# Causal mask inside the vector instruction of the row maxima, and two query tiles scaled ahead of the sine product of the queries, in an attention and soft-expert kernel

## What is computed

```python
q = rope(einsum('bim,mhd->bhid', x, wq)); k = rope(einsum('bim,mhd->bhid', x, wk))
s = einsum('bhid,bhjd->bhij', q, k) / D_HEAD
s = s - INFTY_APPROX * (i < j)              # causal mask: 1e30 where the key is later than the query
p = softmax(s, axis=-1)
o = einsum('bhij,bhjd->bhid', p, v)
x = layernorm(x + einsum('bhid,hdm->bim', o, wo))
```

## Time and profile before

| | us |
|---|---|
| median of 3 runs (lowest, highest) | 2020.32 (2019.03, 2022.83) |
| the profiled execution | 2017.05 |
| its span | 2015.3 |
| PE busy | 1873.9 |
| DVE busy | 1481.6 |
| ACT busy | 1237.2 |
| POOL busy | 1168.8 |

### The profile page before, as it was taken

One profiled execution on the slowest core, in us unless ns is written; L12 is line 12 of the kernel. 1 busy time (PEld: TensorE's weight loads), 2 busy tenths in 40 slices (PEclk: granted clock), 3 DMA queues, 4 the chain that ended last, 5 costly groups with the idle time before them and its releaser, 6 DMA issues. The chain is left out here.

```text
span 2015.3 us, 37894 instructions
## 1 busy us (share of the span) xinstructions
PE 1873.9 (93%) x11126; PEld 1512.8 (75%) x11134; DVE 1481.6 (74%) x2670; ACT 1237.2 (61%) x2543; POOL 1168.8 (58%) x996
## 2 busy tenths in 40 slices
PE   5999999999999999999999999999999968999997
PEld 4777777777777777777777777777777756887886
DVE  4777777777777777777777777777777766777774
ACT  4666666666666666666666666666666644554553
POOL 3666666666666666666656666666666653445543
PEclk8999999999999999999999999999999989999999
DMA  6222322232223222322232223222322230111100
GB/s 201 56 55 86 107 55 55 86 107 55 55 86 107 55 55 86 107 55 55 86 107 55 55 86 107 55 55 86 96 55 55 86 126 22 33 46 38 31 21 22
DMA packets 75415, 142.98 MB, mean 71 GB/s; under 512 B 7936, under 2 KB 42880, under 8 KB 73088
## 3 DMA queue, kind: packets, MB, share of 16 engines
q1 hardware_dynamic: 74208, 141.65, 24.4%
q10 hardware_dynamic: 1184, 1.05, 0.2%
HBM read 16.52 MB, written 8.39 MB: 12 GB/s over the span
## 5 line engine op out<-in xcount | busy, mean ns | idle before, releaser
L397 POOL TENSOR_SCALAR probs<-probs,inv 128x1024 f32<-128x1024 f32 (+7 forms) x514 | 518.5, 1020 | 525.0 <-DVE inv L533 522.2
L432 ACT ACTIVATE probs<-ps_slot,neg_max 128x1024 f32<-128x1024 f32 (+7 forms) x514 | 379.4, 743 | 153.5 <-DVE neg_max L525 153.3
L689 PE MATMUL ps_turn<-ident,probs 128*128 128x128 f32 x2304 | 338.9, 279 | 78.2 <-POOL probs L397 69.4
L525 DVE TENSOR_REDUCE neg_max<-ps_slot 128x1 f32<-128x1024 f32 (+7 forms) x514 | 377.7, 756 | 31.3 <-PE ps_slot L666 20.2
L689 PEld LDWEIGHTS ps_turn<-ident,probs 128*128 128x128 f32 x2304 | 249.9, 141 | 129.3 <-issue 94.5
L664 PE MATMUL ps_slot<-k,q 128*128 128x512 f32 (+3 forms) x772 | 303.2, 393 | 0.0
L659 PE MATMUL ps_slot<-k,q 128*128 128x512 f32 (+3 forms) x772 | 285.8, 370 | 10.1 <-DVE q L551 9.9
L666 PE MATMUL ps_slot<-k,q 128*128 128x512 f32 (+3 forms) x772 | 267.4, 346 | 0.0
L452 ACT ACTIVATE pt_split<-ps_turn 128x512 fp32r<-128x512 f32 x256 | 153.5, 600 | 131.1 <-PE ps_turn L689 129.1
L386 POOL TENSOR_TENSOR rot_k<-unrot_k,rope 128x1024 f32<-128x1024 f32 x64 | 158.1, 2470 | 86.5 <-ACT unrot_k L438 86.5
L558 DVE TENSOR_TENSOR pt_split<-ps_turn,pt_split 128x512 fp32r<-128x512 f32 x256 | 176.2, 688 | 36.8 <-ACT pt_split L452 30.3
(11 more groups left out here) (175 smaller groups left out, 4108.8 us busy)
## 6 DMA issues: line engine op xcount, KB each, us to landing
swapped_q<-unrot_q SPq DMA_DIRECT2D x130, 256.0 KB, 3.8
swapped_k<-unrot_k SPq DMA_DIRECT2D x130, 256.0 KB, 4.5
x_in<-x_t SPq DMA_DIRECT2D x18, 1024.0 KB, 4.6
w_in<-w_all SPq DMA_DIRECT2D x65, 256.0 KB, 2.3
xw_in<-x_whole SPq DMA_DIRECT2D x18, 512.0 KB, 5.7
wvo_in<-wvo_all SPq DMA_DIRECT2D x65, 64.0 KB, 1.9
x_rows<-in_L_attn_x SPq DMA_DIRECT2D x8, 512.0 KB, 5.1
y_t<-y_out SPq DMA_DIRECT2D x8, 512.0 KB, 2.7
```

The source lines that it names most:

```text
L397: pool.tensor_scalar(tile, tile, inv[:, par, stat_col[t]:stat_col[t] + 1], 1.0, ALU.mult, ALU.mult).then_inc(normed, 1)
L432: last = act.activation(probs[:, p_at[t]:p_at[t] + width[t]], src, ACT.Exp, bias=neg_max[:, par, c:c + 1], accum_out=sums[:, par, c:c + 1])
L525: dve.tensor_reduce(neg_max[:, par, c:c + 1], slot(fill, par)[:, i * BANK:i * BANK + width[t]], AX.X, ALU.max, negate=True).then_inc(maxed, 1)
L689: last = pe.transpose(ps_turn[:, bank, at:at + P], probs[:, p_at[t] + j * P:p_at[t] + (j + 1) * P], ident[:, :])
```

## The change

The mask's product on PE and its two bf16 constants are gone. In their place `causal`, a bf16 row of 1024 columns that is 0 and has -1e30 above the diagonal of its last 128 columns, is an operand of `rowmax`: one DVE instruction adds its last 128(t+1) columns to a tile's scores, negates, writes the result back to PSUM and takes the minimum. ACT's exponential has `scale=-1.0` to undo the sign. DVE's wait for `filled` stands in an instruction of its own (`wait_apart`) and DVE waits once for the constants. On POOL, `norm(head_no, par, 4)` moves ahead of `mul_sin(0, head_no + 2)`.

```diff
+        causal = s.sb("causal", [P, T], BF16)
...
+            pool.memset(causal[:, :], 0.0).then_inc(consts, 1)
...
+            pool.affine_select(out=causal[:, T - P:T], in_=causal[:, T - P:T], compare_op=ALU.is_ge, fill=MASKED,
                                base=0, pattern=[[-1, P]], channel_multiplier=1).then_inc(consts, 1)
...
                 norm(head_no, par, 3)
                 mul_sin(1, head_no + 2)
+                norm(head_no, par, 4)
                 mul_sin(0, head_no + 2)
-                norm(head_no, par, 4)
                 norm(head_no, par, 5)
...
-                    last = act.activation(probs[:, p_at[t]:p_at[t] + width[t]], src, ACT.Exp,
+                    last = act.activation(probs[:, p_at[t]:p_at[t] + width[t]], src, ACT.Exp, scale=-1.0,
                                           bias=neg_max[:, par, c:c + 1], accum_out=sums[:, par, c:c + 1])
...
-                dve.wait_ge(filled, head_no * FILLS + fill)
+                wait_apart(dve, filled, head_no * FILLS + fill, dve_ticks)
                 for i, t in enumerate(SLOT_TILES[slot_no]):
                     c = stat_col[t]
-                    dve.tensor_reduce(neg_max[:, par, c:c + 1], slot(fill, par)[:, i * BANK:i * BANK + width[t]],
-                                      AX.X, ALU.max, negate=True).then_inc(maxed, 1)
+                    tile = slot(fill, par)[:, i * BANK:i * BANK + width[t]]
+                    dve.tensor_tensor_reduce(tile, tile, causal[:, T - width[t]:T], -1.0, UNSEEN,
+                                             ALU.add, ALU.min, neg_max[:, par, c:c + 1]).then_inc(maxed, 1)
...
+            dve.wait_ge(consts, 5)
             mul_cos_q(1)
...
-                        if c0 + n == width[t]:
-                            pe.matmul(out[:, n - P:n], ident_b[:, :], mask_b[:, :], start=False, stop=False,
-                                      skip_group_check=True)
```

More of the change, by code:

```diff
@@ L29 @@
 MASKED = -1e30
+UNSEEN = 3e38
 LN_EPS = 1e-5
@@ L245, in attention_block @@
         ident = s.sb("ident1", [P, P], F32)
-        ident_b = s.sb("ident_b", [P, P], BF16)
-        mask_b = s.sb("mask_b", [P, P], BF16)
+        causal = s.sb("causal", [P, T], BF16)
         zeros_b = s.sb("zeros_b", [P, BANK], BF16)
@@ L251, in attention_block @@
         ps_y = s.ps("ps_y", [P, 2, BANK])
-        consts, ticks = s.sem("consts"), s.sem("ticks")
+        consts, ticks, dve_ticks = s.sem("consts"), s.sem("ticks"), s.sem("dve_ticks0")
         x_rows_landed, x_turned = s.sem("x_rows_landed"), s.sem("x_turned1")
@@ L371, in _ @@
             pool.memset(ident[:, :], 0.0).then_inc(consts, 1)
-            pool.memset(ident_b[:, :], 0.0).then_inc(consts, 1)
-            pool.memset(mask_b[:, :], 0.0).then_inc(consts, 1)
+            pool.memset(causal[:, :], 0.0).then_inc(consts, 1)
             pool.memset(zeros_b[:, :], 0.0).then_inc(consts, 1)
             pool.memset(y_out[:, :], 0.0).then_inc(y_free, 1)
[L377 to L381, removed]
+            pool.wait_ge(consts, 3)
+            pool.affine_select(out=ident[:, :], in_=ident[:, :], compare_op=ALU.not_equal, fill=1.0,
+                               base=0, pattern=[[-1, P]], channel_multiplier=1).then_inc(consts, 1)
+            pool.affine_select(out=causal[:, T - P:T], in_=causal[:, T - P:T], compare_op=ALU.is_ge, fill=MASKED,
                                base=0, pattern=[[-1, P]], channel_multiplier=1).then_inc(consts, 1)
@@ L717, in _ @@
             project_v(FIRST, F_V0, 0, 1)
-            pe.wait_ge(consts, 7)
+            pe.wait_ge(consts, 5)
             pe.wait_ge(lo_made[K_ALL], 1)
```

## The result

The changed kernel takes 2187.57 us (median of 4 runs, 2186.57 to 2189.19). The kernel before, run on the same chip, takes 2019.67 us (4 runs, 2018.35 to 2022.83). The ratio is 1.083, with a 95% interval of 1.0811 to 1.0848. The forecast was 2150 in a range from 2070 to 2205; the sign and the places were right, the sum was 38 us short.

A forecast was written before the change was run, and what follows sets the result against it. The prediction took a loop through POOL, DVE, ACT and PE in every head as the bound, not PE alone. 2017 profiled + 76 late chain + 54 clock = 2147, with 3 for the median 2150 us; range 2070 to 2205.

The forecast's parts named there:

- The order on POOL: POOL's queries' product ends 1.9 us later, DVE's keys' sum waits for it; scores +1.65 us a head before masks.
- Where PE stands: PE stands 1.1 us before turn 5 and 1.75 before the scores of slot 0, with 0.7 of work between.
- a small wait of the scores for `q`: Sign of a wrong forecast: PE's wait for DVE's `q` small, so the exclusion or the reciprocal's time is misread.
- The other heads: Last two heads of each batch, 16 in all: between +0.35 and 1.37 us, taken as 0.6 each, 10 us.
- The new instruction: DVE's maxima: the pass costs nothing more, 0.1 us a tile for the second instruction; 6 us in all at 0.2.
- The clock: PE's longer stands bring the lower clock in half the heads, 32 x 1.7 = 54 us; bounds 0 to 109.
- the usual heads: 48 heads whose scores of slot 0 start 1.37 us later, masks taken off: 66 us.
- the masks' own gain: Only the masks of tiles 7 and 6 lie on the loop at PE: 0.28 us a head less.
- B: Rival: the same late chain of keys and queries, but PE's clock stays up; 2096 us, chance 0.24.
- C: Rival: DVE's sum of the keys gets ahead of POOL's queries' product; +0.8 us a head, 2071 us, chance 0.1.
- D: Rival: DVE's new instruction runs at half the rate, about 2.6 us a head more; over 2260 us, chance 0.05.

The follow-up runs named there:

- e3_filled: The changed kernel plus nine products of a zero tile per head where PE stands, four ahead of turn 5, five ahead of its second bank: 2114.11 us.
- e1_join_only: The changed kernel with POOL's old order, both sine products ahead of the scaling of tiles 1 and 0, keeping the joined mask: 2011.44 us.
- e5_queries_only_written: The changed kernel with POOL's sine product of the queries replaced by memsets of nearly the same length that read nothing: 1966.86 us.
- e8_halves_change_order: e1_join_only with the queries' sine product halved, first half between norm 2 and norm 3, second behind norm 4 as in the change's order: 2043.27 us.
- e2_order_only: The kernel before with only POOL's two lines exchanged, norm 4 ahead of the queries' sine product: 2187.02 us.
- e4_no_masks: The kernel before without the mask's products on PE, with its old maxima, leaving the causal mask out: 1998.92 us.
- e7_sum_ahead_of_maxima: e1_join_only, queries' product halved (first half before norm 3), keys' sum ahead of slot 5's maxima, keys' high part ahead of its exponentials: 2062.3 us.

## Why the forecast was right, and where its sum was short

**The order on POOL: right, place by place.** Measured from the start of the keys' product, forecast against measured: the small tiles start at 3.43 and 3.37, the queries' product ends at 6.65 and 6.55, DVE's sum at 7.72 and 7.63, turn 5 starts at 9.15 and 9.23, the scores of slot 0 at 11.60 and 11.72. `e3_filled` less `e1_join_only`, the order without the clock, is 102.7 us or 1.6 a head; in a usual head the scores are 1.77 later (11.72 for 9.95), where the forecast had 1.65 before the masks. `e5_queries_only_written` and `e8_halves_change_order` show the cause itself: no reading, no hold; half the length, 0.94 later for 1.77.

The Trainium skill (SBUF — State Buffer, SBUF: two separate sides) says that a DVE instruction with two inputs in SBUF and a POOL instruction that reads SBUF take a shared pair of ports for their whole length, and that the one that starts first blocks the other. By that rule the trace agrees in each of its parts: wherever POOL's product started first and ran into the sum, the sum ends 1.08 or 1.09 behind it, in all eight kernels in which the two meet as a rule; DVE goes first in one head of the changed kernel and in three of `e2_order_only`; and the memsets have no effect.

**Where PE stands: half right.** The forecast put the second stand in front of the scores, 1.75 us for DVE's `q`. The trace has 1.28, at the second bank of turn 5. The chain is the same, but the wait that comes first was missed: on DVE the copy of turn 4's bank (line 557) stands behind the low part of the keys, and PE needs that half of `ps_turn` before it gets to the scores. The prediction named a small wait of the scores for `q` as a sign that the exclusion or the reciprocal was misread. That sign came (PE's list has such a wait once, in the first head) and was itself wrong: the stand had only moved one step ahead.

**The other heads: a little small.** For the last two of a batch I took 0.6 a head, which is 0.88 before the masks. In heads 46 and 47 the scores stand at 11.19 and 10.98 behind the keys' product, where `e1_join_only` has 9.95: 1.24 and 1.03 more. Sixteen heads at 1.14 in place of 0.88 are 4 us.

**The new instruction: mis-sized.** "Nothing on the loop"; it is 12.5 us, twice the 6 us that the text gave for 0.2 a tile. The pass was priced rightly; the exponential's wait for the second instruction is the likely place of the rest, which is argued and not shown.

**The clock: mechanism right, both factors off.** The forecast was 32 heads at 1.7, 54 us; it is 63 at 1.2, 73.5 us. That the total stayed so near is in part luck: half the heads was a choice between none and all, and too few heads at too high a price err in opposite directions. A piece of 3.41 at half the clock does not cost half of it, in part because it begins in front of the scores: from 1197.60 to 1198.31 PE still stands or turns. The Trainium skill (TensorE: Matmul & The Clock Gate, Why this matters for your kernels) warns only of gaps longer than about 3 us. Where that page and the trace differ, the trace decides: stands of 0.94 and 1.28 with 0.66 of work between them are followed by the lower clock in nearly every head of the changed kernel.

In sum: 94 us without the clock where 76 were forecast, and 74 for the clock where 54 were: 168 for 130. Of the 18 us between 94 and 76, 12.5 are the instruction, 4 the other heads, 6 the usual heads (48 times 0.12) and 3 the difference between the two chips; the masks' own gain, 24 in `e4_no_masks` against 18, takes 6 back. That makes the 18 up to within 2 us. Errors of both signs are in it, and the range of 2070 to 2205 was wide enough for them. Rivals B and C stay out, B because the clock fell (`e3_filled` at 2114 is what B would have been, forecast 2096), C because DVE asks 0.21 behind POOL and not ahead of it. D is out by 699 ns; the profile names the new instruction CUSTOM_DVE_ANT_0, and no run shows whether it is of the family by whose rule the prediction judged D. That the join gives nothing under the new order (2187.57 against 2187.02) was not foreseen; the 16 further falls are of its size.

What decides whether the clock falls stays open. A stand of 1.70 in one piece left it up (`e7_sum_ahead_of_maxima`), one of 1.28 too (`e8_halves_change_order`). One of 1.93 was followed by the lower clock, one of 1.96 in front of 229.77 us of the same trace was not (granted clock 1.00 in the 3.41 us behind it). The pair of 0.94 and 1.28 close together was followed by it in 62 heads of the changed kernel; in `e2_order_only` it was in 44 heads and was not in 17. So the length of the stands alone does not decide it. No kernel varied the work between two stands, or their place in time.

## What to carry to other kernels

When work is moved on POOL, ask what DVE will want to do at the new place: here a long POOL product that reads SBUF, started 0.2 us ahead of DVE's sum of two inputs in SBUF, made the sum end 1.08 us behind POOL's end and delayed all that stands behind it. A short idle time of PE in front of a step need not be the thing to remove; look for an idle time of POOL in which half of the long instruction fits, and split the instruction in two (here 2011 to 1985 us). After a change that makes PE stand, look at the granted clock first: it was 44% of the loss here (73.5 of 168 us).

## What was not expected of the hardware

- Two stands of 0.94 and 1.28 us with 0.66 of work between them were followed by 3.41 us of the lower clock in 62 of 64 heads of the changed kernel, but with only POOL's order changed in 44 of 64; one stand of 1.70 us in each head of `e7_sum_ahead_of_maxima` by none. Filling the two with zero products brought back about 74 us.
- The 1.08 us between POOL's end and the end of DVE's sum were the same for a product of 512 columns as for 1,024, while the sum's bare length is 1.22: most of the sum comes after the release.
- A DVE pass that adds a bf16 SBUF operand to PSUM, writes back and reduces takes as long as the plain reduction (1232 ns against 1225 for 1,024 columns). The separate read behind it takes 141 ns; that the 12.5 us of the new maxima come from it is likely and not shown.
